# Attention with a folded weight product on eight cores: three bias rows moved from TensorE to VectorE, and the product of W1 and W2 spread over the value tiles

## The reference, cut to what matters

```
xn  = layernorm(x)
Q, K, V = xn @ W1 + b1, xn @ W2 + b2, xn @ W3 + b3
attn    = softmax(Q K^T / 32) V @ W4 + b4
W_real, W_imag = 512 x 512 matrices unfolded from small tensors G1, G2
ffn = [xr W_real^T - xi W_imag^T + bias_real, xr W_imag^T + xi W_real^T + bias_imag]   (xr, xi: halves of xn)
out = x + attn + ffn
```

## Time and profile before

| | us |
|---|---|
| median of 3 runs (lowest, highest) | 1292.47 (1292.40, 1293.03) |
| the profiled execution, its own time | 1292.45 |
| its span on the slowest core (core 2) | 1290.9 |
| spans of the eight cores | 1287.7 to 1290.9 |
| granted TensorE clock of the cores | 0.996 to 1.000 |
| TensorE busy | 1268.6 (98%) |
| VectorE, ScalarE, GpSimd busy | 523.0, 329.5, 170.7 |

### The profile page before, as it was taken

One profiled execution on the slowest core, in us unless ns is written; L12 is line 12 of the kernel. 1 busy time (PEld: TensorE's weight loads), 2 busy tenths in 40 slices (PEclk: granted clock), 3 DMA queues, 4 the chain that ended last, 5 costly groups with the idle time before them and its releaser, 6 DMA issues.

```text
span 1290.9 us, 16352 instructions; the slowest of 8 cores (1287.7 to 1290.9 us)
## 1 busy us (share of the span) xinstructions
PE 1268.6 (98%) x6022; PEld 589.2 (46%) x6142; DVE 523.0 (41%) x860; ACT 329.5 (26%) x463; POOL 170.7 (13%) x123
## 2 busy tenths in 40 slices
PE   6999999999999999999999999999999999999998
PEld 4555444444444444444444444444444444444443
DVE  3455671543144414442444343443444244414442
ACT  2453243222211132212122321122212212221111
POOL 2232133211011101111111111111111011101110
PEclk9999999999999999999999999999999999999999
DMA  9889192122222223221222222220233022322222
GB/s 134 195 196 221 39 215 50 34 66 71 60 66 66 66 49 80 68 66 33 66 77 71 49 63 68 66 66 33 72 79 78 34 66 66 66 66 66 66 66 66
DMA packets 178846, 100.74 MB, mean 78 GB/s; under 512 B 160824, under 2 KB 162896, under 8 KB 178768
## 3 DMA queue, kind: packets, MB, share of 16 engines
q1 hardware_dynamic: 173152, 91.28, 29.1%
q0 software_dynamic: 5408, 8.39, 4.4%
q10 hardware_dynamic: 208, 0.02, 0.0%
HBM read 51.43 MB, written 16.78 MB: 53 GB/s over the span
## 4 chain that ended last, share of the span: by engine, by line
PE 98%; DMA 1%; issue 1%; POOL 0%; ACT 0%; DVE 0%; POOLq 0%; ACTq 0%; DVEq 0%
PE ring L795 34%; PE po L837 33%; PE ring L676 9%; PE po L658 4%; PE pf L658 4%; PE pf L822 2%; PE pf L815 2%; PE pf L808 2%; PE po L713 1%; PE ring L645 1%; DMA V<-W 1%; PE po L764 1%; PE pf L764 1%; PE pf L713 1%; PE po L868 1%
## 5 line engine op out<-in xcount | busy, mean ns | idle before, releaser
L795 PE MATMUL ring<-XT,GT 128*128 128x512 bf16 x2004 | 444.9, 379 | 2.5 <-ACT Et L617 0.2
L837 PE MATMUL po<-V,ET 128*128 128x512 bf16 x1945 | 436.1, 379 | 2.1
L795 PEld LDWEIGHTS ring<-XT,GT 128*128 128x128 bf16 x2048 | 200.3, 98 | 242.0 <-issue 0.6
L837 PEld LDWEIGHTS po<-V,ET 128*128 128x128 bf16 x1984 | 194.1, 98 | 234.1
L481 DVE TENSOR_REDUCE mx<-ring 128x1 f32<-128x512 f32 x256 | 176.8, 691 | 222.5 <-PE ring L795 222.4
L507 DVE SCALAR_TENSOR_TENSOR xr<-po,rrv,xr 128x1024 f32<-128x1024 f32 x31 | 39.8, 1284 | 419.7 <-PE po L837 419.7
L329 POOL TENSOR_TENSOR xr<-xr,cb 128x1024 f32<-128x1024 f32 x32 | 75.1, 2346 | 941.9 <-DVE junk L486 941.9
L612 ACT ACTIVATE S<-ring 128x512 f32<-128x512 f32 x128 | 76.4, 597 | 423.7 <-DVE mx L481 423.6
L617 ACT ACTIVATE Et<-ring,ngm 128x2048 bf16<-128x2048 f32 x32 | 63.0, 1967 | 300.6 <-DVE ngm L500 300.6
L676 PE MATMUL ring<-XT,A 128*128 128x512 bf16 x502 | 111.1, 379 | 0.5
L676 PEld LDWEIGHTS ring<-XT,A 128*128 128x128 bf16 x512 | 50.1, 98 | 60.4
(11 more groups left out here) (104 smaller groups left out, 643.0 us busy)
## 6 DMA issues: line engine op xcount, KB each, us to landing
xr<-x SPq DMA_DIRECT2D x40, 512.0 KB, 3.4
out<-xr SPq DMA_DIRECT2D x31, 512.0 KB, 2.7
S<-x SPq DMA_DIRECT2D x16, 512.0 KB, 4.7
Et<-x SPq DMA_DIRECT2D x8, 512.0 KB, 5.1
V<-W POOLq DMA_DIRECT2D x2, 1024.0 KB, 17.3
V<-W POOLq DMA_DIRECT2D x8, 256.0 KB, 18.8
V<-W POOLq DMA_DIRECT2D x4, 512.0 KB, 21.3
A<-W POOLq DMA_DIRECT2D x4, 512.0 KB, 8.4
```

Of the source, the lines that this page charges most:

```text
L795: mm = e.matmul(bank[tb % 4], GT[:, c, rows(i % 4)], XT[:, c, tb * 512:(tb + 1) * 512], start=(c == 0), stop=(c == 7))
L837: mm = e.matmul(po[:, v * 512:(v + 1) * 512], ET[:, i % 2, tj, :], V[:, tj, v * 512:(v + 1) * 512], start=(tj == 16), stop=(tj == 15))
```

## The change

The three vectors are no longer formed by bfloat16 matmuls over all eight row blocks. VectorE sums weight rows over the eight blocks, each row scaled by its bias element (`row_op`: one operation on 128 x 1024 per block, 24 in all, into float32 accumulators `accb`, `accu`, `accc`), and the sum over the 128 partitions is then made on TensorE by float32 matmuls with a matrix of ones: one of 128 x 128 by one column for each block of W2 b1 (`small_c`, 8 and one more for b1 . b2), and two of 128 x 512 each for the other two rows (`u_row`, `b_row`). The eight blocks of A stand in the steps k = 13 to 20, one in front of each value tile, in the banks 2 and 3 and evicted in halves. W1 is turned wholly by transposing DMAs (at SyncE's k = 11, 13, 15, 17), and x tiles from tile 8 on by transposing DMAs (NPE 12 to 8). W2's transpose lies in the last quarter of `XT`, so that SyncE waits before tile 24 for the whole of A and for `accc`. The `weight_op`s stand in steps 18 to 29, where they stood in the stage of A and steps 16 to 22. The loads of b4 and the ffn biases are at k = 24 and 30.

```diff
-AFOLD = 16
-NPE = 12
+AFOLD = 13
+NPE = 8
...
-    W2T = V[:, 16:24, :]
+    W2T = XT[:, :, 3072:4096]
+    accb, accu, accc = cb[:, :], ub[:, :], xr[:, 1, :]
+    ones = XS[:, 2:4, :].rearrange("p a n -> p (a n)").bitcast(F32)
...
-    fold = ([(m, 0) for m in range(4)] + [(8, 0), (8, 1)] + [(m, 1) for m in range(4)]
+    fold = ([(m, 0) for m in range(4)] + [(m, 1) for m in range(4)]
...
     def sync_program(e):
             if k >= NPE:
+                if k == 24:
+                    e.wait_ge(s_am, 16)
+                    e.wait_ge(s_accc, 8)
                 e.dma_start_transpose(XT[:, :, rows(k)], xnn[k % 2]).then_inc(d_xt[k % 2], 16)
...
-            if k in (13, 14):
-                if k == 13:
+            if k in (11, 13, 15, 17):
+                p = (k - 11) // 2
+                if p == 0:
                     e.wait_ge(s_w2tp, 8)
...
-            if k == 18:
+            if k == 24:
+                e.wait_ge(s_cm, 1)
                 (load of b4)
-            elif k == 27:
+            elif k == 30:
...
     def gpsimd_program(e):
+        e.memset(ones, 1.0).then_inc(s_ones, 1)
-            elif k in (4, 6, 7, 9):
+            elif k in (4, 5, 6, 7):
...
     def vector_program(e):
+        def row_op(acc, w, b, done, j):
+            col = bcol[:, b + j:b + j + 1]
+            if j == 0:
+                e.wait_ge(s_rep, 1)
+                e.tensor_scalar(acc, w[:, 0, :], col, None, ALU.mult).then_inc(done, 1)
+            else:
+                e.wait_ge(done, j)
+                e.scalar_tensor_tensor(acc, w[:, j, :], col, acc, ALU.mult, ALU.add
+                                       ).then_inc(done, 1)
...
-        for s in range(2):
-            e.tensor_copy(rep[:, s], bps[:, 8 * s + 8:8 * s + 16].unsqueeze(2)
-                          .broadcast_to([128, 8, 128])).then_inc(s_rep, 1)
...
-        for k in range(AFOLD):
+        for k in range(NT):
             step(k)
+            if 9 <= k < 13:
+                row_op(accb, W4raw, 16, s_accb, k - 9)
+            elif 13 <= k < 16:
+                (four a step: accb 4 to 7, then accc 0 to 7 from W2T)
+            elif 16 <= k < 21:
+                (four a step: accu 0 to 7 from W1T, then weight_op 7 to 18)
+            elif 21 <= k < 30:
+                weight_op(k - 2)
+            if k == 20:
+                (b12: product of b1 and b2 with its sum, then_inc(s_accc, 1))
+            elif k == 21:
+                (cc, then ub from the banks, then su)
+            elif k == 26:
+                (cb = b_row's banks + b4)
...
     def scalar_program(e):
+            if AFOLD <= k < AFOLD + 8:
+                for n in (2 * (k - AFOLD), 2 * (k - AFOLD) + 1):
+                    e.wait_ge(s_am, n + 1)
+                    e.activation(A[:, k - AFOLD, 512 * (n % 2):512 * (n % 2 + 1)],
+                                 bank[2 + n % 2], AF.Identity).then_inc(s_ae, 1)
...
     def tensor_program(e):
+        def small_c():
+            e.wait_ge(s_ones, 1)
+            e.wait_ge(s_accc, 9)
+            for m in range(8):
+                e.matmul(bank[0][:, m:m + 1], accc[:, rows(m)], ones[:, 0:1],
+                         start=True, stop=True)
+            e.matmul(bank[0][:, 8:9], ones, b12[:, 8:9], start=True, stop=True
+                     ).then_inc(s_cm, 1)
+        def u_row():
+            e.wait_ge(s_accu, 8)
+            for h in range(2):
+                e.wait_ge(s_ae, 15 + h)
+                e.matmul(bank[2 + h], ones, accu[:, 512 * h:512 * (h + 1)],
+                         start=True, stop=True).then_inc(s_ubm, 1)
+        (b_row: the same with accb, in banks 0 and 1, behind s_accb 8 and s_c 1)
...
+        for k in range(NT - 1):
+            for g in step_groups(k):
                 turn(g)
+            if AFOLD <= k < AFOLD + 8:
+                a_block(k - AFOLD)
             if k == NT - 2:
                 g_group(0)
             v_half(k, 0)
             v_half(k, 1)
+            if k == AFOLD + 7:
+                small_c()
+                u_row()
+            elif k == AFOLD + 9:
+                b_row()
```

More of the change, by code:

```diff
@@ L167, in build_nc @@
     s_id, s_nsc, s_lnap, s_wsum, s_cba = sem("id"), sem("nsc"), sem("lnap"), sem("wsum"), sem("cba")
-    s_xs = sem("xs")
+    s_xs, s_ones = sem("xs"), sem("ones")
     d_g1 = [sem("d_g1r"), sem("d_g1i")]
     d_g2, d_bb, d_bc = sem("d_g2"), sem("d_bb"), sem("d_bc")
-    d_w1t = sem("d_w1t")
+    d_w1t = [sem(f"d_w1t{k}") for k in range(4)]
     d_w2 = [sem(f"d_w2{k}") for k in range(4)]
@@ L406, in vector_program @@
         e.wait_ge(s_g1x, 2)
-        weight_ops(0, 7)
+        for n in range(7):
+            weight_op(n)
         evict_group(("w3", 4))
@@ L582, in scalar_program @@
         evict_group(("w3", 3))
-        evict_w34(2, 9)
+        evict_w34(2, 7)
         evict_group(("w3", 5))
-        evict_w34(9, 10)
+        evict_w34(7, 8)
         ln_rstd(0)
+        evict_w34(8, 10)
+        ln_rstd(1)
         evict_w34(10, 12)
-        ln_rstd(1)
-        evict_w34(12, 14)
         evict_group(("w3", 7))
         ln_rstd(2)
-        evict_w34(14, 18)
+        evict_w34(12, 16)
         ln_rstd(3)
         evict_group(("xn", 1))
[L595 to L601, removed]
+        for k in range(NT - 1):
             step(k)
@@ L712, in fold34 @@
                 for j in range(8):
-                    mm = e.matmul(obank[n % 4],
-                                  W3T[:, j, rows(m)] if m < 8 else b3rep[:, j, :],
-                                  W4half[h][:, j, :], start=(j == 0), stop=(j == 7))
+                    mm = e.matmul(obank[n % 4], W3T[:, j, rows(m)], W4half[h][:, j, :], start=(j == 0), stop=(j == 7))
                 mm.then_inc(s_w34m, 1)
@@ L723, in tensor_program @@
         turn(("w3", 3))
-        fold34(2, 8)
+        fold34(2, 6)
         turn(("w3", 4))
-        fold34(8, 9)
+        fold34(6, 7)
         turn(("w3", 5))
-        fold34(9, 12)
+        fold34(7, 10)
         turn(("w3", 6))
+        fold34(10, 12)
+        turn(("w3", 7))
         fold34(12, 14)
-        turn(("w3", 7))
-        fold34(14, 16)
         turn(("xn", 0))
-        fold34(16, 17)
+        fold34(14, 15)
         turn(("xn", 1))
[L736 to L740, removed]
-                turn(g)
-            v_half(k, 0)
-            v_half(k, 1)
@@ L746, in tensor_program @@
[L746 to L750, removed]
-                e.matmul(bank[2][:, m:m + 1], W2T[:, j, rows(m)], b1c[:, j:j + 1],
-                         start=(j == 0), stop=(j == 7))
-        for j in range(8):
-            mm = e.matmul(bank[2][:, 8:9], b2rep[:, j, :], b1c[:, j:j + 1],
-                          start=(j == 0), stop=(j == 7))
-        mm.then_inc(s_cm, 1)
@@ new lines, in u_row, with b_row @@
+        def u_row():
+            e.wait_ge(s_accu, 8)
+            for h in range(2):
+                e.wait_ge(s_ae, 15 + h)
+                e.matmul(bank[2 + h], ones, accu[:, 512 * h:512 * (h + 1)],
+                         start=True, stop=True).then_inc(s_ubm, 1)
+        def b_row():
+            e.wait_ge(s_accb, 8)
+            e.wait_ge(s_c, 1)
+            for h in range(2):
+                e.matmul(bank[h], ones, accb[:, 512 * h:512 * (h + 1)],
+                         start=True, stop=True).then_inc(s_bm, 1)
@@ new lines, in a_block @@
+        def a_block(m):
+            e.wait_ge(d_w1t[m // 2], 32)
+            for h in range(2):
+                if m >= 1:
+                    e.wait_ge(s_ae, 2 * m + h - 1)
+                elif h == 0:
+                    for b in range(2):
+                        e.wait_ge(s_pt[b], (len(groups) - 1 - b) // 2 + 1)
+                for j in range(8):
+                    mm = e.matmul(bank[2 + h], W1T[:, j, rows(m)],
+                                  W2T[:, j, h * 512:(h + 1) * 512],
+                                  start=(j == 0), stop=(j == 7))
+                mm.then_inc(s_am, 1)
@@ L778, in tensor_program @@
+        for k in range(NT - 1):
+            for g in step_groups(k):
+                turn(g)
+            if AFOLD <= k < AFOLD + 8:
+                a_block(k - AFOLD)
             if k == NT - 2:
```

139 lines of the change are left out of this document (58 added, 81 removed).

## The result

| | before | after |
|---|---|---|
| median, 10 runs each on the same chip | 1293.01 us | 1296.13 us |
| profiled execution, its own time | 1292.45 | 1294.88 |
| span of the slowest core | 1290.9 (core 2) | 1293.3 (core 6) |
| granted TensorE clock of the cores | 0.996 to 1.000 | 0.992 to 0.997 |

The ratio is 1.0025, 95% interval 1.0016 to 1.0034: 3.2 us slower, not 4.65 faster. (Ratios leave disturbed executions out; the profiled execution of one experiment, e6, had one die disturbed, and of it only cores 0 to 3 are read.)

A forecast was written before the change was run, and what follows sets the result against it. TensorE's own work was taken as the bound, busy 1268.6 of 1290.9 us. Its work falls by 12.5 - 4.0 - 3.45 = 5.05 us, less a 0.4 wait: 4.65, from 1292.45 to 1287.8 us; 8-in-10 range 1284.9 to 1292.6.

The forecast's parts named there:

- TensorE's own work: Prologue: loses 12.5 us of matmuls and turns, gains 4.0 and 3.45 of float32 matmuls, so falls by 5.05 us.
- the column: `small_c` on TensorE: nine float32 matmuls, 18 records of 0.22 us, 4.0 us added.
- the two rows: `u_row` and `b_row` on TensorE: four float32 matmuls of 512 columns, 8 records of 0.43 us, 3.45 us added.
- the rival of cheap short matmuls: `small_c` costs only 0.5 to 2 us, giving 1284.3 to 1285.8 us; chance 0.12.
- the eight turns: Transposes of x tiles 8 to 11 and W1 blocks 0 to 3 leave TensorE: 0.45 us each, 3.6 saved.
- 0.22 us a record: Pace of float32 matmul records on TensorE, taken as set by loading of float32 weights; used to price `small_c`.
- b3 W4: Product at the start, 16 matmuls removed from TensorE; 3.45 us saved, counted in full as W4's half lands 1.3 early.
- the filler rival: The b3 product only filled time until W4's second half landed: at most 3.45 us back, 1291.3 us; chance 0.06.
- the wait is about 0.4 us: TensorE at `small_c` waits for VectorE's `b12`, last work of step 20, done at 58.9 against TensorE's 58.7.
- up to twice 1.73: SyncE queue cost, in us, of a pair of W1's transposing DMAs; the added DMAs were costed at nothing.
- the slower rival: VectorE bounds steps 13 to 20, GpSimd's normalizations holding it up: 9.6 us later, 1297.4 us; chance 0.11.
- the wait counts in full: At `small_c`, `u_row` and tile 21 stand behind the wait on TensorE, so its 0.4 us adds fully.

The follow-up runs named there:

- e6: Kernel of e1 with the nine float32 column matmuls done twice in a row, no wait; ratio 0.9982 to the kernel before.
- e1: Changed kernel with VectorE's small product b1 . b2 made in step 15, not behind the unfolding's operations of steps 18 to 20; 1285.02 us, ratio 0.9945.
- e8: Kernel of e1 with x tiles 8 to 11 turned on TensorE again, not by transposing DMAs; 1287.07 us, ratio 0.9967.
- e9: Changed kernel, product b1 . b2 still late, with x tiles 8 to 11 turned on TensorE, not by transposing DMAs; ratio 0.9996.
- e5: Kernel of e1, but TensorE waits behind value tile 20 for VectorE's step 20, then does a dense tile before the float32 matmuls; 1292.60 us, ratio 1.0005.
- e7: Changed kernel with three unfolding operations a step in steps 18 to 20 instead of four, two a step in 21 to 23; 1287.28 us, ratio 0.9968.
- e4: Changed kernel with W1's eight transposing DMAs one a step at SyncE's k = 11 to 18, not in pairs; ratio 1.0016.

## Why the prediction was wrong

**TensorE's own work: mechanism right, one term twice too large.** In e1, where nothing disturbs it, the column takes 1.93 us (forecast 4.0), the two rows 1.80 + 1.72 = 3.5 (forecast 3.45). So the rival of cheap short matmuls (0.5 to 2 us) had the column's price right. The distance from the first value tile to the first `GT` group fell from 145.86 us (core 0 before) to 142.47 (e1). From the rows: b2 W1^T 3.45, W2 b1 2.02 and the eight turns 3.56, less 1.93 + 1.80 + 1.72, are 3.6; measured 3.4. With the fold of b3 that makes about 7 us where I had forecast 5.05, and e1 is 7.1 us faster than the kernel before.

**The pace of the thin float32 matmuls.** I read 0.22 us a record from the earlier trace rows, gave it to the loading of weights, and it is 0.106 at full clock (1.70 us for 16 in e1) and 0.213 at half (3.40 us for 16 in the changed kernel). The first matmuls of the kernel before run at nearly the half-clock pace, though the profile's granted clock is 1.00 there. It looks as if I had read an engine at half clock for one at full clock. That column of the profile can't be relied on so early: on core 2 before, eight bfloat16 matmuls of 128 x 512 from 18.91 us take 22.32 - 18.91 = 3.41 us, 0.43 each and so twice the later 0.216, where it says 1.00; on core 0 the same eight take 3.42 where it says 0.50. For the first float32 matmuls themselves it isn't shown. The column in the changed kernel cost 3.82 us, near my 4.0, by luck: that is twice the 1.93 of full clock.

**The start gave back some of b3 W4.** The first value tile begins at 52.8 us (median of the eight cores; before 54.9, e1 51.9): 2.1 and 3.0 us of 3.45. The load of W4's second half was in time on most cores; on core 2 TensorE waited 1.4 us for it. On every core 0.6 to 1.9 us went to a wait that I hadn't seen: the eviction of a transpose of W3, which stands in VectorE's program behind the statistics of late x tiles. So the filler rival, with up to 3.45 us back, has something of the size, but for most of it another mechanism.

**The step that failed: "the wait is about 0.4 us".** It was 4.2. TensorE came to that place when it was forecast to (101.36 + 58.7 = 160.06, measured 164.40 - 4.17 = 160.23), and steps 14 to 20 on VectorE took 163.86 - 114.22 = 49.6 us where 7 x 7.1 = 49.7 was forecast. The latter is partly luck: row operations in a chain stand 1.39 us apart in place of 1.33, but the first of each sum has no second tensor to read and took only 0.75. But VectorE began step 13 at 105.54, 4.2 us behind tile 11 in place of 1.8, and step 13 took 8.7 us in place of 7.1: 2.4 + 1.6 = 4.0 us. The 1.8 itself was right: e8 and e9, where VectorE waits for no x load, show 1.8 on most cores. I had costed the added DMAs at nothing after checking only when value tiles are wanted, and had their time on the queue too small: "up to twice 1.73" for a pair of W1, where the first pair took 3.9 to 4.5 us and the second 4.9 to 6.3 on the eight cores. From the first pair to the second SyncE needed 100.31 - 92.12 = 8.2 us for two steps, forecast 7.1, where TensorE needs 6.9. The queue's other customers are VectorE, whose x loads stand behind the pairs, and GpSimd, whose normalizations then meet row operations. The mechanism of the slower rival was in the trace as described, one row operation of 2.03 us at a late normalization. The Trainium skill, "SBUF — State Buffer", section Who interferes with whom, has the shared port held by whoever comes first, for the whole instruction, and the rows agree, turn by turn: GpSimd's began at 109.60 beside VectorE's second operation (109.49 to 110.78) and ended at 111.84, and VectorE's third, from 110.88, took 2.03 us. This collision cost VectorE about 0.75 us there and 0.2 to 0.3 at single ones, not 9.6, and x loads cost more.

**What I didn't have at all: the clock.** I wrote that the wait counts in full; on the profiled core it counted double. Behind it the column ran at half clock (3.82 for 1.93), the row W1 b2 too (3.56 for 1.80), and tile 21 took 4.12 for 3.45: 4.3 us. Shown by e1 (no wait, none of it), e5 (a wait alone) and e6 (thin matmuls alone). The Trainium skill, "TensorE: Matmul & The Clock Gate", section The HAM clock gate, knows the two clocks and names half as the idle one; the windows agree (0.50 and 1.00). I should have priced a stop of TensorE at either level.

In sum, against the forecast on the profiled core: wait + 3.8, row W1 b2 + 1.8, tile 21 + 0.7, column - 0.2, start + 0.7 (from 56.8 us on core 2 before, where the first record of the tile is missing, to 54.1 on core 6, 2.7 of 3.45), together 6.8 of the 1294.88 - 1287.8 = 7.1 us. All of it but the start hangs on one instruction's place in VectorE's program, as e1 shows.

What stays open: how much of VectorE's lateness is x loads and how much collisions (e8 and e9 still have the long row operations of step 13, some 6.2 us for four, and yet e9's wait is 1.4 us at most, so the loads seem to weigh more); whether in e9 it is the missing DMAs or the 0.45 us that each turn adds to steps 6 to 9, in which loads can land; and why two cores with nearly the same wait part ways in clock.

## What to carry to other kernels

When TensorE is the bound and at full clock, a wait on its path costs itself and then a loss of clock: in front of dense work waits of 3.4 to 5.9 us cost another 1.6 to 2.6 (e5), in front of thin float32 matmuls waits of 2.5 to 5.3 us another 3.4 to 5.0 (the changed kernel). Hide such sums behind dense work, and let nothing that is cheap stand in another engine's order behind something long. Put an instruction whose result is awaited right behind its inputs, not at the end of a step: here that was worth 10 us. A moved DMA must be checked for everyone who stands behind it on the queue, not only for its own consumer.

## What the runs showed of the hardware

- A float32 matmul shows two records. With 512 columns a record takes 0.43 us at full clock (1.72 us for four, the row at 179.35) and 0.89 at half (3.56 us for four, the row at 168.22); with one column 0.106 (1.70 us for 16, e1) and 0.213 (3.40 us for 16, the changed kernel).
- A stretch of one-column float32 matmuls, in which the profile calls TensorE wholly busy, lowered the granted clock in 3.8 us (e6, three of four cores), and not in 1.9 us (e1, all cores).
- The clock fell behind a wait of 0.5 us directly ahead of such matmuls on a core of e7, while it stayed behind 1.2 us on one of e9; 2.6 us ahead of dense work cost 1.8 us more on one core of e5 and 0.2 on another.
- VectorE's row operation on bfloat16 weights with a float32 accumulator takes 1.28 us and in a chain one starts every 1.39; one that met GpSimd's normalization took 2.03, and that one 2.24 in place of 1.20 (the changed kernel, core 6).
- A pair of transposing DMAs of 128 x 1024 bfloat16 back to back held SyncE's queue for 3.4 to 6.3 us in the changed kernel, where single ones in e4 took 1.2 to 2.9, most of them under 1.4.
